# A delta-rule attention layer with a routed feed-forward layer: three operations of ScalarE put elsewhere in its step

## What is computed

```python
def step(S, inp):
    q_t, k_t, v_t, b_t = inp
    pred = jnp.einsum('bhk,bhkv->bhv', k_t, S)
    delta = (v_t - pred) * b_t[..., None]
    S = S + k_t[..., :, None] * delta[..., None, :]
    o_t = jnp.einsum('bhk,bhkv->bhv', q_t, S)
    return (S, o_t)
...
o = o * jax.lax.rsqrt(jnp.mean(o * o, axis=-1, keepdims=True) + EPS) * norm_w
o = o * (g * jax.nn.sigmoid(g))
return o.reshape(b, n, H * DV) @ Wo
```

## Time and profile before

| what | value |
|---|---|
| time, median of 3 runs | 524.82 us (523.22 to 527.61) |
| the profiled execution, its own time | 524.84 us |
| its span, first to last instruction | 523.1 us |
| mean granted PE clock in the span | 0.97 of full speed |
| PE busy | 467.4 us (89%) |
| ACT busy | 327.8 us (63%) |
| DVE busy | 314.9 us (60%) |
| POOL busy | 292.2 us (56%) |

### The profile page before, as it was taken

How to read it: one execution, slowest core, us unless ns; L and a number is a source line. 1 busy time by engine, 2 the same in 40 slices (tenths; PEclk the granted TensorE clock), 3 DMA queues, 4 the chain that set the end, 5 groups by cost and what they waited for, 6 DMA issues and landing times.

```text
span 523.1 us, 19041 instructions
## 1 busy us (share of the span) xinstructions
PE 467.4 (89%) x7181; PEld 389.0 (74%) x7181; DVE 314.9 (60%) x1209; ACT 327.8 (63%) x905; POOL 292.2 (56%) x445
## 2 busy tenths in 40 slices
PE   6979999999999999999898988999999999999900
PEld 4656766777667776776665677999999999999900
DVE  4435467667686676766875764644555545555345
ACT  3545668877888778878675634555555555555463
POOL 3055517638377383682753341567777767767652
PEclk9998999999999999999997999999999999999965
DMA  3367763552335514336161113354655545553376
GB/s 96 32 113 186 217 172 58 111 90 33 71 50 85 84 26 77 51 54 99 31 174 42 34 47 93 47 112 55 119 107 77 111 56 123 95 82 32 31 151 201
DMA packets 148084, 46.10 MB, mean 88 GB/s; under 512 B 107168, under 2 KB 141600, under 8 KB 148000
## 3 DMA queue, kind: packets, MB, share of 16 engines
q1 hardware_dynamic: 132848, 29.86, 29.0%
q0 software_dynamic: 13568, 9.51, 13.1%
q10 hardware_dynamic: 1584, 5.59, 2.8%
HBM read 21.39 MB, written 23.55 MB: 86 GB/s over the span
## 4 chain that ended last, share of the span: by engine, by line
PE 69%; issue 9%; ACT 9%; DMA 7%; DVE 2%; SPq 2%; POOL 1%; ACTq 0%; DVEq 0%; POOLq 0%
PE ps L1004 17%; PE ps L1015 11%; PE ps L730 5%; PE ps L681 4%; ACT TT L1126 3%; PE ps L684 2%; PE ps L761 2%; PE ps L737 2%; PE ps L812 2%; PE ps L881 2%; PE ps L896 2%; PE ps L800 2%; PE ps L1030 2%; PE ps L870 2%; PE ps L842 2%
## 5 line engine op out<-in xcount | busy, mean ns | idle before, releaser
L1784 POOL DMA_INDIRECT x_store<-xk,row x80 | 125.7, 1571 | 65.0 <-ACT xk L1275 45.5
L1603 DVE TENSOR_TENSOR hb<-ps,hs 128x320 f32<-128x320 f32 (+1 forms) x128 | 62.5, 491 | 44.6 <-ACT hs L1267 44.0
L1744 POOL DMA_INDIRECT slots_in<-x,slot x64 | 63.5, 992 | 25.4 <-issue 16.6
L1267 ACT ACTIVATE hs<-ps 128x320 f32<-128x320 f32 (+1 forms) x128 | 55.2, 435 | 32.0 <-PE ps L1004 31.2
L1004 PE MATMUL ps<-xeTh,w13h 128*128 128x320 f32 x224 | 70.5, 315 | 1.0 <-DVE xeTl L1627 1.0
L1004 PE MATMUL ps<-xeTh,w13l 128*128 128x320 f32 x224 | 69.2, 309 | 0.0
L1004 PE MATMUL ps<-xeTl,w13h 128*128 128x320 f32 x224 | 69.1, 309 | 0.0
L1015 PE MATMUL ps<-w2s,hb 128*128 128x128 f32 x512 | 64.3, 278 | 0.1
L1015 PEld LDWEIGHTS ps<-w2s,hb 128*128 128x128 f32 x512 | 59.8, 192 | 2.2 <-DVE hb L1603 0.3
L1757 POOL TENSOR_TENSOR Vk<-V,sq 128x256 f32<-128x256 f32 x16 | 10.4, 647 | 86.7 <-ACT sq L1109 86.6
L1275 ACT ACTIVATE xk<-ps,gs 128x128 f32<-128x128 f32 x80 | 24.2, 364 | 44.9 <-PE ps L1030 35.3
(11 more groups left out here) (218 smaller groups left out, 1147.5 us busy)
## 6 DMA issues: line engine op xcount, KB each, us to landing
slots_in<-zeros ACTq DMA_DIRECT2D x10, 520.0 KB, 4.2
xe<-slots_in SPq DMA_DIRECT2D x15, 325.0 KB, 2.9
w<-w_in SPq DMA_DIRECT2D x8, 448.0 KB, 4.3
xTs<-xT SPq DMA_DIRECT2D x4, 512.0 KB, 5.5
a_diag<-hb SPq DMA_DIRECT2D x64, 32.0 KB
inv<-xs SPq DMA_DIRECT2D x16, 128.0 KB
xi<-inv SPq DMA_DIRECT2D x16, 128.0 KB
xk<-x SPq DMA_DIRECT2D x8, 256.0 KB, 3.6
```

Source lines behind the costliest of these rows:

```text
L1267: af(hs[to, s % 4, :], ps[src, HB[fill_of(s) % 5], 0:HALF], ACT.Silu).then_inc(hs_ready, 1)
L1603: v.tensor_tensor(hb[to, par, c, HALF * g:HALF * g + HALF], ps[rows_, at, 0:HALF], hs[rows_, s % 4, :], ALU.mult).then_inc(h_ready, 1)
L1744: g.indirect_dma_start(out=xs_d[:, :], out_offset=bass.IndirectOffsetOnAxis(ap=to, axis=0), in_=x1[:, p % 2, j, k, :], in_offset=None,).th ...
L1784: g.indirect_dma_start(out=x1_d[:, :], in_=ye[:, par, i, :], in_offset=None, out_offset=bass.IndirectOffsetOnAxis(ap=row[:, par, i:i + 1], ...
```

## The change

Three calls move inside ACT's step. No instruction is added or taken away, no wait is changed, and no other engine's list changes.

```diff
             for p in range(NP + LAST):
+                at(z128_copy, p - 7)
                 at(key_key_out, p - 3, 0)
-                at(z128_copy, p - 7)
                 at(queries_out, p - 6, 0)
...
                 clear(p, 0)
+                at(deltas_turned, p - 7)
                 at(queries_out, p - 6, 1)
-                at(deltas_turned, p - 7)
                 at(softmax, p - 8)
...
+                at(keys_out, p - 2, 0)
                 at(head_norms, p - 7)
...
                 at(t_diag, p - 6)
                 clear(p, 3)
-                at(keys_out, p - 2, 0)
                 at(keys_out, p - 2, 1)
```

## The result

The changed kernel takes 545.94 us (median of 4 runs, 544.71 to 551.37), against 525.07 us of the kernel before in the same comparison (4 runs): a ratio of 1.0408, with a 95% interval of 1.0363 to 1.0453. It is slower, by some 21 us. The forecast was 542.5 us, within 535 to 549. The profiled execution took 544.71 us, with a span of 542.9 us; that of before is 19.8 us shorter in span.

What follows compares the result with a forecast made beforehand. PE was taken to nearly fill the step, with waits for ACT deciding. Terms +1.70 (p' = 6), +6.8 (7 to 10), +9.8 (11 to 17) and -0.6 behind gave +17.7 on 524.8: 542.5 us, range 535 to 549.

Steps and rivals of the forecast that it cites:

- The wait: ACT's first half of `y` waits for `state_keys` ahead of the heads' norms: 1.75 us lost per step, p' = 7 to 17.
- p' = 6: First step where `y` waits for `state_keys`; the half moves ahead of `TT` only, `key_pair` 1.70 us later.
- The rival by which the copy fits in the gap (A): `y` finds its wait over and runs in ACT's idle 1.37 us: some 7 us faster, 517.5 us; chance 0.03.
- `z`: `z` ahead of `hb` on ACT: PE's `w_128` waits less, 0.25 us gained per step, p' = 11 to 18.
- `dl`: `dl` ahead of the second `gq` on ACT: PE's `outputs` start sooner, at most 0.14 us, taken as 0.10.
- the reading of `z_32`'s end: On PE, `z_32` runs from 190.89 to 191.62 and `outputs` starts at 191.76, so `dl` gains at most 0.14 us.
- Rival C: The clock falls in PE's new idle time: another 2.7 us a step, 30 us in 11, 572 us; chance 0.04.
- If the clock of the loop falls under 1.00: Sign of being wrong: the attention loop's granted clock was to stay at 1.00.
- The step sum of the forecast for p' = 7 to 17: Losses less gains in the 11 steps with heads' norm and keys' copy: 6.8 us plus 9.8 us.
- The steps behind p' = 17: Steps without a keys' copy: -0.25 us once and -0.10 three or four times, together -0.6 us.
- B: PE's and DVE's work closes up while ACT is late: only about 1 us lost per step, 537 us; chance 0.10.
- D: No change: gains cancel the loss or the step has unseen slack, 522 to 529 us; chance 0.03.

Runs made afterwards that it cites:

- The run with this edit alone: Only the first half of the keys' copy moved ahead of the heads' norms, against the kernel before; 557.68 us, ratio 1.0631.
- the five slots: The changed kernel with a ring of five slots for y in place of four; 517.57 us, ratio 0.9862 against the kernel before.

## Why the prediction was right

Slower was forecast for the reason that the trace shows, and the time lies in the range. Step by step:

**The wait.** Counted from `head_sums` (156.94 in the rows of the changed kernel): the first half of `y` starts 2.39 us later (forecast 2.38), the second half 5.40 (5.41), `w_64` 3.90 (3.95), `key_pair` 6.26 (6.26). The run with this edit alone has a step of 18.30 us, just 1.75 above 16.55. The whole step came out at 17.80 us and not at 18.2: the forecast started from a step of 16.8 us, one of the longer ones (16.55 is the sixth), and its gains were 0.15 us too low. At p' = 6 the shift is as forecast too; the rows of the changed kernel are

```profile
46.03 0.65 PE L826 MATMUL ps<-y,Zs 128*32 128x128 f32 x16
...
49.85 0.61 PE L730 MATMUL ps<-y,xTs 128*64 128x512 f32 x1 [1.77 <-ACT y L1070]
```

From the end of `state_keys` (46.68) to `key_pair` it is 3.17 us, and before it was 47.17 - 45.70 = 1.47, a difference of 1.70.

The rival by which the copy fits in the gap (A) fell, and for the reason given; the five slots make that rival's condition true and give 517.57 us, where it was priced at 517.5. Its full step gains 0.82 us by them, where 0.7 was priced, so the near equality of the totals is in part chance.

**The two gains.** `z` was put at 0.25 and brought 0.30. `dl` was put at 0.10, from "at most 0.14", and brought 0.16 to 0.22. The step that failed is the reading of `z_32`'s end: the row's 0.73 us runs to the modelled end of the last of 64 matmuls, but the next group starts 0.66 us after the first. What follows a train of matmuls on PE is better read from start to start.

**The clock.** Rival C had a chance of 0.04 as a cost of every step. It happened in part, in four of eleven. "If the clock of the loop falls under 1.00" was also one of the prediction's own signs of being wrong: the forecast had put the clock at no cost, and that part of it failed. The step sum of the forecast for p' = 7 to 17 was 6.8 + 9.8 = 16.6 us; the profile has 203.9 - 184.2 = 19.7. The seven steps without a fall lost 1.24 to 1.67 us each, 9.7 in all or 1.39 on average, where 16.6 / 11 = 1.51 was forecast; the four with a fall lost 2.34 to 2.76, 10.0 in all. So a fall cost about 1.1 us more, not the 2.7 that I priced. The misses went against each other: the four falls added some 4.4 us, apart from them the eleven steps lost 1.3 us less than forecast, and the steps behind them (below) gave back 1.5 us more than forecast. That the median lies 3.4 us from the forecast is therefore partly luck. One of the four runs, at 551.37 us, lies outside the range, and their mean granted clocks differ (0.953 to 0.963); whether that is more falls in the loop no trace shows.

The clock fell during PE's idle time before `key_pair` or within 0.4 us behind it, as the rival had it: in the fall at 198 us PE had been idle about 1 us before `w_64` and 0.79 before `key_pair`. The seven other steps have idle stretches of the same length and no fall; what tells these apart is open. The Trainium skill ("TensorE: Matmul & The Clock Gate", section "HAM oscillation — how this bites in real kernels") describes a loop in which the wait for data in every iteration is longer than the work, and in which every iteration starts at the lower clock. This loop is another case: its idle time is about 2 us of a step of 17.8, and the trace shows the clock fall in some steps only.

**The rest of the sum.** The steps behind p' = 17 were put at -0.6 us with the last `z`; from the twelfth `head_sums` to the last the profile has 56.35 us against 58.49, that is -2.1. Before, the clock's fall and the stall at 275 stood in one of these steps; they stand in another now. The first `head_sums` came 2.48 us later: `state_keys` of p' = 6 was already 0.98 late (46.03 against 45.05), p' = 6 added 1.70, and 0.2 was made up after it. So the span's account is 2.5 + 19.7 - 2.1 - 0.2 = 19.9, against 19.8 measured. These ends differ from run to run (55.54 us from the twelfth `head_sums` to the last in the kernel before with five slots, 58.49 with four) and were only bounded in the forecast, with two or three us for stalls.

**B and D.** Nothing closed up: the loss of a step in the run with the keys' copy alone is the whole 1.75 us. The gains did not cancel it either.

## What to carry to other kernels

Idle time of an engine is usable only by an instruction whose waits are over there: before a copy into a ring is moved ahead, look up who reads the slot last, and where that reader stands in its own engine's order. Where the reader comes later than the gap, one more slot moves the wait a whole step back, and the same order that lost 4% gains 1.4%. And when an engine that runs close to full is made to idle, look at the granted clock of those stretches too, since the loss can be larger than the wait.

## What was not expected of the hardware

In the kernel before, a single stall of 1.42 us had no such effect. With four extra matmuls per step in the second of the two stretches, 1.05 us of work, it stayed up in every step, though the stretch before `w_64` was as long as before (0.99 us). With `state_keys` earlier most steps kept only a stretch of 0.5 to 0.8 us before `key_pair`, and the clock stayed up as well. These are one profile each.
